# The second attention's query products in 64x64 tiles, two heads at a time, and their copies in halves

## The reference

```
def _L1_attn_ref(x, Wq, Wk, Wv, Wu, bu):
    EMB, HEADS, K = (64, 8, 32)
    scale = e ** 0.25
    xp = jnp.pad(x, ((0, 0), (k - 1, 0), (0, 0)))
    q = (x @ Wq.T).reshape(b, t, h, e) / scale
    kk = (xp @ Wk.T).reshape(b, tp, h, e) / scale
    v = (xp @ Wv.T).reshape(b, tp, h, e)
    idx = jnp.arange(t)[:, None] + jnp.arange(k)[None, :]
    dot = jnp.einsum('bthe,btkhe->bthk', q, kk[:, idx])
    attn = jax.nn.softmax(dot, axis=-1)
    out = jnp.einsum('bthk,btkhe->bthe', attn, v[:, idx])
    return out.reshape(b, t, h * e) @ Wu.T + bu
```

## Time and profile before

| | us |
|---|---|
| three timed runs, median | 560.37 |
| lowest and highest of them | 547.56 and 560.54 |
| the profiled execution's own time | 545.75 |
| its span, first to last instruction | 543.8 |
| TensorE busy in it | 463.1 (85%) |
| VectorE busy | 327.1 (60%) |
| ScalarE busy | 282.3 (52%) |

### The profile page before, as it was taken

The page is one execution under the profiler, slowest core; times in us unless marked ns, Lnnn a source line. Parts: engine busy times, 40 slices in busy tenths (PEclk is TensorE's granted clock), DMA queues, the critical chain, the costliest instruction groups (busy, mean ns, idle before and its releaser), DMA issues.

```text
span 543.8 us, 7830 instructions
## 1 busy us (share of the span) xinstructions
PE 463.1 (85%) x3219; PEld 176.0 (32%) x3219; DVE 327.1 (60%) x604; ACT 282.3 (52%) x472; POOL 11.0 (2%) x14
## 2 busy tenths in 40 slices
PE   7768898988899898787899897899998988995884
PEld 2421222232233332232234332222333323542483
DVE  2569787789648653689468554696332545524414
ACT  2410476755773465564862563738864754172242
POOL 8000000000000000000000000000000000000000
PEclk9875699998999999999998999989999999997897
DMA  8685000007100000027000000000000000000003
GB/s 292 133 157 84 1 1 3 1 0 145 30 2 1 2 1 1 1 46 129 0 2 1 2 1 1 2 0 1 1 2 1 1 1 1 2 1 0 1 1 79
DMA packets 7476, 15.41 MB, mean 28 GB/s; under 512 B 1424, under 2 KB 4496, under 8 KB 7312
## 3 DMA queue, kind: packets, MB, share of 16 engines
q1 hardware_dynamic: 7440, 14.90, 12.5%
HBM read 10.61 MB, written 4.19 MB: 27 GB/s over the span
## 4 chain that ended last, share of the span: by engine, by line
PE 61%; DVE 22%; ACT 10%; DMA 3%; issue 2%; SPq 1%; DVEq 0%; ACTq 0%
DVE part_max L1083 9%; PE O L671 7%; PE R L719 5%; PE T L658 4%; PE T L638 4%; PE R L828 3%; PE R L658 3%; PE R L638 3%; PE R L597 3%; PE R L789 2%; PE R L605 2%; PE R L816 2%; PE R L803 2%; ACT rlog L985 2%; ACT probs L954 2%
## 5 line engine op out<-in xcount | busy, mean ns | idle before, releaser
L954 ACT ACTIVATE probs<-T 128x512 f32<-128x512 f32 x159 | 90.9, 596 | 81.4 <-PE T L658 80.9
L1083 DVE TENSOR_REDUCE part_max<-T 128x1 f32<-128x512 f32 x153 | 100.6, 683 | 36.6 <-PE T L638 36.5
L954 ACT ACTIVATE probs<-R 128x512 f32<-128x512 f32 x97 | 55.7, 596 | 46.8 <-PE R L658 46.5
L1083 DVE TENSOR_REDUCE part_max<-R 128x1 f32<-128x512 f32 x103 | 68.7, 683 | 9.8 <-PE R L638 9.7
L638 PE MATMUL T<-KX,QX 96*128 96x512 bf16 x153 | 63.4, 428 | 8.6 <-DMA KX<-qk_scratch 4.5
L671 PE MATMUL O<-probs,VT 128*32 128x512 f32 x512 | 67.7, 604 | 1.1 <-ACT probs L954 1.1
L658 PE MATMUL T<-QX,KX 99*128 99x512 bf16 x159 | 59.5, 393 | 3.5 <-DMA QX<-mx_part 2.6
L638 PE MATMUL R<-KX,QX 96*128 96x512 bf16 x103 | 42.5, 423 | 2.7 <-DVE part_max L1083 2.7
L658 PE MATMUL R<-QX,KX 99*128 99x512 bf16 x97 | 36.0, 388 | 1.4 <-DMA QX<-mx_part 1.2
L719 PE MATMUL R<-xp,abd 128*128 128x512 f32 x64 | 32.0, 603 | 1.2 <-DVE xp L1057 1.2
L638 PEld LDWEIGHTS T<-KX,QX 96*128 96x128 bf16 x153 | 15.0, 100 | 47.4 <-DVE part_max L1083 25.1
(11 more groups left out here) (210 smaller groups left out, 622.6 us busy)
## 6 DMA issues: line engine op xcount, KB each, us to landing
qk_scratch<-qk_part SPq DMA_DIRECT2D x8, 384.0 KB, 4.5
zs<-early SPq DMA_DIRECT2D x1, 2048.0 KB, 7.9
QX<-qk_scratch SPq DMA_DIRECT2D x4, 384.0 KB, 4.9
KX<-qk_scratch SPq DMA_DIRECT2D x4, 384.0 KB, 6.9
QX<-qk_scratch SPq DMA_DIRECT2D x4, 256.0 KB, 7.6
KX<-qk_scratch SPq DMA_DIRECT2D x4, 256.0 KB, 8.5
result<-probs SPq DMA_DIRECT2D x2, 512.0 KB, 5.2
s_rest<-rest SPq DMA_DIRECT2D x1, 882.0 KB, 10.2
```

The lines of the kernel that those rows point to most:

```text
L954: A(probs[:, u % 2, h, :], ring["scores", b, u, h], ACT.Exp, scale=HD ** -0.5).then_inc(g["exp_done"], 1)
L1083: nc.vector.tensor_reduce(part_max[:, row, kh:kh + 1], ring["max_piece", b, half, i], AX_X, ALU.max).then_inc(g["max_red"], 1)
```

## The change

Each head's fp32 matmul of 128x128 goes. In its place an even and an odd head are made together in four matmuls of 64x64, which take only the corners of `abd` that aren't zero. The even head of the first half of the positions goes from input partitions 0 to 63 to output partitions 0 to 63 of the first of two banks, its second half from 64 to 127 to 64 to 127 of the second bank; the odd head goes across, first half to partitions 64 to 127 of the first bank, second half to 0 to 63 of the second bank. So each of the four corners of TensorE's array has one of the matmuls, as `unify` has it. A pair fills two banks: `z_pairs(b)` is one for batches 0 to 2 and two for batch 3. ScalarE copies each head in two instructions of 64 partitions, one for each half of the positions. A pair waits until both heads of the pair that had its banks are copied. `z_mm` now counts pairs, `z_copied` still heads.

```
-                if h >= z_banks(b):
-                    pe.wait_ge(g["z_copied"], b * H1 + h - z_banks(b) + 1)
-                mm(R[:, h % z_banks(b), :], abd[:, h, :], xn, start=True, stop=True).then_inc(g["z_mm"], 1)
+                if h % 2:
+                    return
+                if h >= 2 * z_pairs(b):
+                    pe.wait_ge(g["z_copied"], b * H1 + h + 2 - 2 * z_pairs(b))
+                for odd in range(2):
+                    for half in range(2):
+                        last = mm(z_bank(b, h, half)[half_rows(odd ^ half), :], abd[half_rows(half), h + odd, half_rows(half)],
+                                  xn[half_rows(half), :], start=True, stop=True)
+                last.then_inc(g["z_mm"], 1)
...
             def tokens(b, r):
 
-                pe.wait_ge(g["z_copied"], b * H1 + H1 - z_banks(b) + 1 + r)
+                pe.wait_ge(g["z_copied"], b * H1 + H1 + 2 - 2 * z_pairs(b))
...
             def queries(b, h):
-                act.wait_ge(g["z_mm"], b * H1 + h + 1)
-                A(z[:, :, h, :], R[:, h % z_banks(b), :].rearrange("p (i q) -> p i q", q=W), ACT.Copy).then_inc(g["z_copied"], 1)
+                act.wait_ge(g["z_mm"], (b * H1 + h) // 2 + 1)
+                for half in range(2):
+                    last = A(z[half_rows(half), :, h, :], z_bank(b, h, half)[half_rows(h % 2 ^ half), :].rearrange("p (i q) -> p i q", q=W),
+                             ACT.Copy)
+                last.then_inc(g["z_copied"], 1)
```

```
+        def z_bank(b, h, half):
+            return R[:, (h // 2 % 2 * 2 if b == B - 1 else 0) + half, :]
+
+        def z_pairs(b):
+            return 2 if b == B - 1 else 1
```

More of the change, by code:

```diff
@@ L469, in win_bank @@
             return R[:, 2:4, :] if b == B - 1 and r % 2 == 0 else R[:, 0:2, :]
-        def z_banks(b):
-            return 4 if b == B - 1 else 2
+        def z_bank(b, h, half):
+            return R[:, (h // 2 % 2 * 2 if b == B - 1 else 0) + half, :]
+        def z_pairs(b):
+            return 2 if b == B - 1 else 1
         def rden1(b, r):
```

## The result

The changed kernel takes 574.38 us (median of four runs, 570.99 to 579.74), the kernel before 553.96 beside it (545.6 to 560.54): 20 us less. The ratio, 1.0488 with a 95% interval of 1.0314 to 1.0661, goes by the fast runs of both kernels, 573.25 against 546.58 us on average, and is larger than that of the medians, 1.037, since two of the four runs of the kernel before lie at 560. The profiled executions stand 25.3 us apart in span: 569.1 us after, 543.8 before, with mean granted clocks of 0.929 and 0.944.

A forecast was written before the change was run, and what follows sets the result against it. TensorE was taken to bound all four query stretches. Batches 0 to 3 were to add 3.65 + 3.65 + 2.9 + 2.0 = 12.2 us to the median of 560.4, giving 572.6 us, range 554 to 579.

The forecast's parts named there:

- What TensorE saves: Queries: a pair of heads takes 1.10 us instead of 1.72, saving 0.62 us a pair, 2.5 us a batch.
- Rival 4: Queries: the 64x64 matmuls aren't run four at a time, 3.4 us a pair, well over 590 us; chance 0.02.
- What ScalarE pays: Queries: eight added copies a batch at 0.605 us, 4.8 us, more than the 4.05 or 2.6 ScalarE had left.
- The walk: Queries to tokens or windows, followed in program order through TensorE and ScalarE: +3.65, +3.65, +2.9 and +2.0 us by batch.
- The wait that is added: Batches 0 to 2: each next pair waits for four copies, so TensorE and ScalarE take turns; +3.65, +3.65, +2.9 us.
- Rival 1: Queries, not slower: copies start 0.49 us apart, as exps do; 7.8 us more, 568 us, 1.4%; chance 0.33.
- Rival 2: Queries, a gain: waits covered, only TensorE counts, tail stays at +2.0; -5.5 us, 555 us; chance 0.07.
- Nothing recovered: Stages behind the queries: all their work starts later in a fixed order, so no delay is counted as taken back.
- Rival 3: Stretches behind the queries, slower still: the granted clock falls after TensorE's idle, 4 to 5.5 us, some 577 us; chance 0.18.

The follow-up runs named there:

- the kernel that reads low: The changed kernel, with every copy reading partitions 0 to 63 of its bank and still writing z's own half; one run, 570.91 us.

## Why the prediction was right or wrong

The time came out within the range and 2 us from the number, but that is luck in two errors of opposite sign. What the change does was forecast as 12.2 us and is 25 us in the profiles, 20 in the medians. The mechanism of the forecast, more copies in turns with TensorE, was right, but two steps of the sum failed. The clock was put at nothing and cost 6.7 us in the first trace (6.3, and 0.4 in batch 3's tokens). The spacing of 0.49 us where an exp and a copy meet was wrong, for 2.2 us. Some 4 us more stay open. The base was too high: I took the median of three runs, 560.4, over the profiled 545.75; with more runs the kernel before has medians of 547.4 to 547.9 in the three later sets of runs. With the right base my sum would have given 560.

**What TensorE saves: right.** A pair takes 1.09 us busy, its result is with ScalarE 1.16 after its start (forecast 1.15), and TensorE's busy time in batch 0's stretch fell from 12.17 to 9.69, by 2.5 us, as worked out. Rival 4 is excluded by the same row.

**What ScalarE pays: a step failed.** 0.605 between copies is right (four in 2.42, sixteen in 9.73). "Where an exp and a copy meet I take 0.49" is wrong: three of four such meetings cost 0.60 to 0.63 (at the fourth the copy waits for its result), because a copy that reads or writes from partition 64 has no overlap with its neighbours on either side. The walk shows it piece by piece. Pair 1 came 3.63 us after pair 0, exactly as walked, since there are only copies in it; pair 2 after 7.87 instead of 7.63; pair 3 after 12.12 instead of 11.63; tokens after 16.49 instead of 15.87. In batches 0 to 2 the miss is 0.64 + 0.64 + 0.95 = 2.23 us. Batch 3 has no exps between its copies; its miss of 0.52 is the clock in the tokens for 0.41 and only 0.1 in the walk (11.49 us at the full clock, 11.40 forecast). Together it is 2.75 us, and 12.2 became 14.95. The row that I leant on, abd at 16.01, had two copies next to each other and no exp; I used it for what it showed and the exps' row for what neither showed.

**The wait that is added: right, and the core of it.** TensorE stands still before three of four pairs for 1.22, 2.18 and 1.66 us and 1.75 before the tokens, all released by ScalarE's z. The pairs with whole copies show that the wait costs nothing when a pair needs only two copies, 1.09 us; halved copies alone cost 0.2 us in batch 0, 0.5 up to the windows. Only the two together cost 4.3.

**Rival 1: wrong in the machine, close in its sum.** The copies don't start 0.49 apart. When they were made to, the stretches cost 2.62, 2.62, 1.78 and 0.66, in all 7.68 us; its walk had 2.5, 2.5, 2.1 and 0.7, in all 7.8. The 0.7 doesn't follow from its own numbers, though: copies until 467.21, 0.42 for the cast and 0.14 to the windows are 467.77, +0.3. That the measured tail is 0.66 is chance.

**Rival 2** had the right reason against it, ScalarE's own sum. With whole copies, where that sum stays as it was, the stretches do gain 5.6 us, but nearly half of it (2.48) in batch 3, where the rival had a loss.

**Nothing recovered: right.** No stretch behind the queries got shorter by more than 1.1 us.

**Rival 3, the clock: this is the step that failed by size.** I left it out of the sum, at 0.18, with 4 to 5.5 us. It came true beside the forecast, not instead of it. In the first trace 6.3 us, in the second 7.7 us stand in tokens and windows with unchanged code; 0.4 us in batch 3's tokens and, in the second, 1.8 us in batch 1's queries come on top. With the waits of batches 0 to 2 filled it is gone from the tokens there, so the idle turns have a part in it; the kernel that reads low shows that they needn't bring it at this place. The evidence was already in my own walk (idle waits of 1.3 to 2.1 us where there had been 0.03 us of idle in 12.20) and in the earlier trace rows, where the kernel before loses its clock twice. It should have been a term of the sum with a chance over one half.

**Not settled.** Of the first profile's 25.3 us some 4 remain in stretches whose code and order haven't changed, in the second nothing on balance. Start to queries 0 varied from 155.4 to 159.9 us over the kernels that change nothing there except by a few fills; and filling every wait in batches 0 to 2 lowered the span by 3.8 us only, the clock falling elsewhere. The runs show that the falls move when anything upstream moves; what puts each of them at its place they don't show. For the timed runs that lie well above their profiles (560.37 and 560.54 against 545.75 us before, 577.71 and 579.74 against 570.99 after) there is no trace.

## What to carry to other kernels

Here, splitting a product into smaller tiles shortened its stretches (by 5.6 us, though hardly the whole) only where what it writes was evacuated in as many instructions as before: count the evacuations first, and if both copies and waits grow, walk the two engines, since the two together cost far more than either alone. Lay the outputs out so that each evacuation starts at partition 0 with all 128 partitions. When a change puts idle time into a stretch in which TensorE had none, price the clock as part of the forecast, and don't take a base from three runs that spread by 13 us.

## What the runs showed of the hardware

- **In these runs ScalarE overlapped consecutive instructions only where both started at partition 0.** Activations of 512 fp32 columns start 0.48 to 0.50 us apart when they and the one ahead read and write from partition 0, with 64 or 128 partitions alike, and 0.59 to 0.63 when either reads or writes from partition 64. Two in a row with the same start at 64 didn't occur. The Trainium skill (ScalarE: Activation LUTs, What ACT_TABLE_LOAD costs) says back-to-back ACTIVATEs overlap by some 93 ns; the runs show 0.11 us (0.60 less 0.49) in the first case and none in the second.
- **64 partitions cost what 128 do.** Copies of 64x512 take 0.58 to 0.60 us, of 128x512 0.60.
- **Idle time in one stage can be paid in the next.** The stretch with 9.69 busy of 16.5 us ran at clock 1.00, and the granted clock behind it was 0.64 over 4.7 us; with the idle filled by dummy matmuls it was 1.00, and the pairs' fillers cost the stretch nothing (16.49 both times). In the kernel that reads low the tokens behind 16.04 us of such turns took 3.32 us all the same.
- **The falls move.** Two executions of one kernel had them in different places, and fillers in batch 3 moved one from the tokens into the windows at nearly the same price (21.87 instead of 22.24 us).
